# A mixture-of-experts loop that takes its token rows by transposing transfers instead of turning them on TensorE

## The reference

```python
x = x + tanh(g_xattn[0]) * _L0_xattn_ref(ctx_1024, _layernorm(x), ...)
x = x + tanh(g_ffn[0])   * _L0_ffn_ref(_layernorm(x), ...)      # experts
x = x + tanh(g_xattn[1]) * _L1_xattn_ref(_layernorm(x), ctx_1024, ...)
x = x + tanh(g_ffn[1])   * _L1_ffn_ref(_layernorm(x), w1, w2)

def _L0_ffn_ref(...):                       # 2048 tokens, 16 experts, 2 per token
    scores = sigmoid(x @ gate_w); _, selected = top_k(scores + expert_bias, 2)
    top_scores = scores of the two, divided by their sum
    shared = silu(x @ shared_gate_w) * (x @ shared_up_w) @ shared_down_w
    comb = zeros((T, E)).at[arange(T)[:, None], selected].add(top_scores)
    for e in range(16):
        g, u = split(x @ experts_gate_up[e], 2)        # 512 -> 2 x 256
        routed += comb[:, e:e + 1] * (silu(g) * u @ experts_down[e])   # 256 -> 512
    return shared + routed
```

## Time and profile before

| what | value |
|---|---|
| median of 3 runs | 1572.79 us (1571.97 to 1574.34) |
| profiled execution, its own time | 1561.98 us |
| its span | 1560.2 us |
| its mean granted TensorE clock | 0.972 |
| PE busy over the span | 1442.6 us, 92% |
| ACT, DVE, POOL busy | 967.2, 1111.0, 634.1 us |
| tile loads `e_xg` | 47 of 256 KB, median 2.7 us from issue to landing |

### The profile page before, as it was taken

One profiled execution on the slowest core, in us unless ns is written; L12 is line 12 of the kernel. 1 busy time (PEld: TensorE's weight loads), 2 busy tenths in 40 slices (PEclk: granted clock), 3 DMA queues, 4 the chain that ended last, 5 costly groups with the idle time before them and its releaser, 6 DMA issues. The chain is left out here.

```text
span 1560.2 us, 21493 instructions
## 1 busy us (share of the span) xinstructions
PE 1442.6 (92%) x6244; PEld 629.0 (40%) x6245; DVE 1111.0 (71%) x1628; ACT 967.2 (62%) x1544; POOL 634.1 (41%) x412
## 2 busy tenths in 40 slices
PE   5698988988988999999999999699999999999999
PEld 2344434434444444444444444123333333244444
DVE  7989999999996422222222488899999999647985
ACT  3999998999974001111111254478788788877764
POOL 0689799698981630064646565240000000000000
PEclk7799999999999999999999999699999999999999
DMA  5212314113205485357833566352322322220465
GB/s 188 72 48 84 94 55 119 44 56 109 75 15 197 155 203 187 128 182 238 288 128 100 187 211 163 108 175 74 96 75 73 94 77 73 60 108 14 88 141 122
DMA packets 137850, 183.45 MB, mean 118 GB/s; under 512 B 55491, under 2 KB 83523, under 8 KB 136755
## 3 DMA queue, kind: packets, MB, share of 16 engines
q1 hardware_dynamic: 113846, 123.83, 27.8%
q0 software_dynamic: 9024, 33.89, 7.0%
q10 hardware_dynamic: 14912, 24.89, 4.9%
HBM read 109.29 MB, written 54.92 MB: 105 GB/s over the span
## 5 line engine op out<-in xcount | busy, mean ns | idle before, releaser
L1916 DVE TENSOR_REDUCE a_mx<-a_s 128x2 f32<-128x1024 f32 x256 | 303.4, 1219 | 34.3 <-PE a_s L2033 31.4
L283 POOL TENSOR_TENSOR m_hs<-m_hs,m_C 128x1024 f32<-128x1024 f32 x128 | 301.5, 2377 | 53.9 <-DVE m_hs L508 53.2
L508 DVE TENSOR_TENSOR_SCAN m_hs<-m_dA,m_d 128x512 f32<-128x512 f32 x256 | 294.6, 1201 | 12.3 <-PE m_d L663 11.2
L663 PE MATMUL m_d<-ident_sb,m_dBuT 128*128 128x128 f32 x1024 | 160.2, 291 | 16.3 <-DVE m_hs L508 8.3
L389 ACT ACTIVATE m_dA<-m_dt,m_negA 128x512 f32<-128x512 f32 x256 | 167.8, 711 | 11.4 <-DMA m_dt<-m_dt 11.3
L663 PEld LDWEIGHTS m_d<-ident_sb,m_dBuT 128*128 128x128 f32 x1024 | 117.4, 146 | 141.5 <-DVE m_hs L508 69.7
L1357 PE MATMUL e_gu<-e_w,e_xgT 128*128 x376 | 169.1, 592 | 0.0
L367 ACT ACTIVATE m_dBuT<-m_dtuT,m_BT 128x512 f32<-128x512 f32 x241 | 157.8, 711 | 0.2
L2033 PE MATMUL a_s<-ring_sb 96*128 96x512 bf16 x512 | 152.3, 390 | 6.0 <-DVE a_mx L1916 4.3
L678 PE MATMUL m_y<-m_hs,m_fold 128*64 128x512 f32 x512 | 142.4, 637 | 3.6 <-POOL m_hs L283 3.6
L2307 POOL MEMSET f_ones<- 128x128 f32 x1 | 0.2, 204 | 343.7 <-POOLq L1500 343.7
(11 more groups left out here) (349 smaller groups left out, 2455.7 us busy)
## 6 DMA issues: line engine op xcount, KB each, us to landing
e_w<-in_ex_gu SPq DMA_DIRECT2D x16, 1024.0 KB, 6.3
ring_sb<-qk_dram SPq DMA_DIRECT2D x64, 192.0 KB, 3.1
xg_dram<-zeros_sb SPq DMA_DIRECT2D x47, 256.0 KB, 3.1
e_xg<-xg_dram ACTq DMA_DIRECT2D x47, 256.0 KB, 2.7
yg_dram<-attn_sb ACTq DMA_DIRECT2D x47, 256.0 KB, 2.1
m_C<-c_dram SPq DMA_DIRECT2D x64, 128.0 KB, 2.9
m_dt<-m_dt SPq DMA_DIRECT2D x64, 128.0 KB, 2.4
e_w<-in_ex_dn SPq DMA_DIRECT2D x16, 512.0 KB, 7.6
```

Source lines behind the costliest of these rows:

```text
L283: pool.tensor_tensor(hs[:, J % RH], hs[:, J % RH], C2[:, N % RC].unsqueeze(1).broadcast_to([P, 2, L]), ALU.mult).then_inc(s_hc, 1)
L508: dve.tensor_tensor_scan(hs[:, J % RH, h], dA[:, j % RA], pd[j % RD][:], 0.0, ALU.mult, ALU.add)\
L663: last = pe.transpose(pd[j % RD][:, t * P:(t + 1) * P], dBuT[:, N % 2, t, g], ident[:])
L1916: dve.tensor_reduce(mx[:, r % 2, h * TB + 2 * c:h * TB + 2 * c + 2], psc[c][:], AX.X, ALU.max)\
```

## The change

The rows reach `xgT` without PE. The scattered rows are stored as two planes of 16-bit numbers: POOL first copies every `xn` tile to a plane pair, the low halves of the 512 values and then the high halves (`planes`, 16 copies; tile 0 goes into `xgT`, tile t into the place of `xn` tile t - 1). `xg_dram` holds 1024 16-bit values in a row, the same 2 KB. ACT loads a tile by a transposing transfer, and its copy joins low and high halves into 512 float32 values. PE's `fetch` is gone; ACT copies tile j + 2 after the silu of tile j, where it had copied tile j + 1. ACT's loop is written out, PE's and DVE's stay loops. The four early loads become 16 pieces of 128 to 256 KB in another order (wk, context, wv, wq), each bound to a tile's end and to the landing of the piece before it.

```diff
+        xp = sb("xp", [P, 2, 2 * KD, P], U16)
-        xg = sb("xg", [P, 2, D])
+        planes = [xgT[:, 0].rearrange("p k t -> p (k t)")] + [xn[:, t] for t in range(NT - 1)]
@@ POOL, ahead of the scatter
+            for t in range(NT):
+                pool.wait_ge(s_xn, t + 1)
+                if t >= 1:
+                    pool.wait_ge(s_xt, t)
+                    pool.wait_ge(s_pl, t)
+                pool.tensor_copy(planes[t].bitcast(U16).rearrange("p (h d) -> p h d", h=2),
+                                 xn[:, t].bitcast(U16).rearrange("p (d h) -> p h d", h=2)).then_inc(s_pl, 1)
+            pool.wait_ge(s_pl, NT)
@@ POOL, loads of the projections' weights
-            for src, kn, width in ((a["ctxT"], KC, T), (a["wv"], KC, D), (a["wk"], KC, D), (a["wq"], KD, D)):
-                pool.dma_start(early[:, at:at + kn * width].rearrange("p (k e) -> p k e", k=kn),
-                               src.rearrange("(k p) e -> p k e", p=P)).then_inc(s_early, 16)
+            def load_early(n, name, k, width, col=0):
+                pool.wait_ge(s_y, NT + 1 + 2 * n)
+                if n >= 1:
+                    pool.wait_ge(s_early, 16 * n)
+                to = at[name] + k * (T if name == "ctxT" else D) + col
+                pool.dma_start(early[:, to:to + width], a[name][k * P:(k + 1) * P, col:col + width]).then_inc(s_early, 16)
+            EARLY = [("wk", k, D) for k in range(KC)] + [("ctxT", k, L, b * L) for b in range(B) for k in range(KC)] + \
+                [("wv", k, D) for k in range(KC)] + [("wq", k, D) for k in range(KD)]
             for m in range(2 * B):
+                first = 0 if m == 0 else KEYS_FROM + 2 * m
+                for n in range(first, min(KEYS_FROM + 2 * m + 2, len(EARLY))):
+                    load_early(n, *EARLY[n])
                 key_rows(m)
@@ ACT
             def load(j, par):
-                act.dma_start(xg[:, par], xg_dram[bass.ds(j, 1)].rearrange("o p d -> (o p) d"))\
-                    .then_inc(s_ld[par], 16)
+                act.dma_start_transpose(xp[:, par], xg_dram[j]).then_inc(s_ld[par], 16)
             def tile(j, par, more=True):
-                act.wait_ge(s_xt, NT + 1 + j)
+                act.wait_ge(s_ld[par], 16 * (j // 2 + 1))
                 act.wait_ge(s_gu, NB + j - 1)
-                act.activation(xgT[:, par], pxt[par][:], ACT.Copy).then_inc(s_xtc, 1)
+                act.activation(xgT[:, par].bitcast(U16).rearrange("p k (t h) -> p h k t", h=2),
+                               xp[:, par].rearrange("p (h k) t -> p h k t", h=2), ACT.Copy).then_inc(s_xtc, 1)
                 if more:
+                    act.wait_ge(s_xtc, NT + j + 1)
                     load(j + 2, par)
             tile(0, 0)
+            tile(1, 1)
             act.wait_ge(s_hm, NB)
             silu(0, 0)
-            tile(1, 1)
+            tile(2, 0)
             def pair(i):
                 for m in range(2):
                     silu(i * 2 + (m + 1), (m + 1) % 2)
-                    tile(i * 2 + (m + 2), m)
+                    tile(i * 2 + (m + 3), 1 - m)
                     store(i * 2 + m, m)
@@ PE
-            def fetch(j, par, nload):
...
             def step(i, m, before, e):
                 turn(i * 2 + (m - 1), (m - 1) % 2)
                 routed_up(i * 2 + m, m % 2, e)
-                if not last:
-                    fetch(i * 2 + (m + 1), (m + 1) % 2, (i + (m + 1) // 2) * 16 + 16)
                 routed_down(i * 2 + (m - 1), (m - 1) % 2, before)
             def key_block(b, f):
                 pe.wait_ge(s_kc, b * KD + (f + 1))
+                if f == 0:
+                    pe.wait_ge(s_early, b * 16 * KC + 16 * (KC + KC))
```

More of the change, by code:

```diff
@@ L14 @@
 U8 = mybir.dt.uint8
+U16 = mybir.dt.uint16
 ALU = mybir.AluOpType
@@ L199, in load_c @@
                     sp.dma_start(xg_dram[j].rearrange("p (c d) -> p c d", c=2),
-                                 zeros[:].unsqueeze(1).broadcast_to([P, 2, D // 2])).then_inc(s_zero, 16)
+                                 zeros[:].bitcast(U16).unsqueeze(1).broadcast_to([P, 2, D])).then_inc(s_zero, 16)
             def zeroed(N):
@@ L859, in moe @@
         s_slot = sem("slots_ready")
+        s_pl = sem("rows_in_halves")
         s_ej = sem("tile_experts")
@@ L959, in _ @@
                                             bass.IndirectOffsetOnAxis(ap=slot[:, k, t:t + 1], axis=0),
-                                            xn[:, t, :], None).then_inc(s_sct, 16)
+                                            planes[t].bitcast(U16), None).then_inc(s_sct, 16)
             pool.wait_ge(s_sct, 16 * 2 * NT)
@@ L967, in _ @@
             pool.wait_ge(s_y, NT)
[L968 to L972 removed]
+            at = {"ctxT": 0, "wv": KC * T, "wk": KC * T + KC * D, "wq": KC * T + 2 * KC * D}
+            def load_early(n, name, k, width, col=0):
[6 more added lines that the diff above has]
+                [("wv", k, D) for k in range(KC)] + [("wq", k, D) for k in range(KD)]
             def key_rows(m):
@@ L1087, in copy_key @@
                 act.activation(raw[:, f // 2, f % 2], pkm, ACT.Copy).then_inc(s_kc, 1)
-            with act.Fori(0, KEYS_FROM) as i:
+            for i in range((ST - 5) // 2):
                 pair(i)
[L1091 to L1094, removed]
-            for i in range(KEYS_FROM + KD * B, (ST - 5) // 2):
-                pair(i)
+                if 0 <= i - KEYS_FROM < KD * B:
+                    copy_key(*divmod(i - KEYS_FROM, KD))
             for j in range(ST - 3, ST):
                 silu(j - 1, (j - 1) % 2)
-                tile(j, j % 2, more=(j < ST - 2))
+                if j + 1 < ST:
+                    tile(j + 1, (j + 1) % 2, more=(j + 1 < ST - 2))
                 store(j - 2, j % 2)
@@ L1401, in _ @@
                 shared_down(t)
-            def fetch(j, par, nload):
-                pe.wait_ge(s_ld[par], nload)
-                if not (isinstance(j, int) and j < 2):
-                    pe.wait_ge(s_xtc, NT + j - 1)
-                for k in range(KD):
-                    last = pe.transpose(pxt[par][:, k], xg[:, par, k * P:(k + 1) * P], ident[:])
-                last.then_inc(s_xt, 1)
             def routed_up(j, par, e):
@@ L1423, in expert, with step, pair @@
                 return pe.value_load(ej[0:1, bass.ds(j, 1)], min_val=0, max_val=NE - 1)
-            def step(i, m, before, e, last=False):
+            def step(i, m, before, e):
                 turn(i * 2 + (m - 1), (m - 1) % 2)
                 routed_up(i * 2 + m, m % 2, e)
-                if not last:
-                    fetch(i * 2 + (m + 1), (m + 1) % 2, (i + (m + 1) // 2) * 16 + 16)
                 routed_down(i * 2 + (m - 1), (m - 1) % 2, before)
-            def pair(i, last=False):
+            def pair(i):
                 before, e1 = expert(i * 2), expert(i * 2 + 1)
@@ L1438, in pair @@
                 e2 = expert(i * 2 + 2)
-                step(i, 2, e1, e2, last)
-            fetch(0, 0, 16)
+                step(i, 2, e1, e2)
             shared_down(NT - 2)
@@ L1444, in _ @@
             routed_up(0, 0, expert(0))
-            fetch(1, 1, 16)
             shared_down(NT - 1)
@@ L1456, in _ @@
                 pair(i)
-            pe.wait_ge(s_early, 16 * 4)
             with pe.Fori(0, B) as b:
@@ L1463, in _ @@
                 pair(i)
-            pair((ST - 1) // 2 - 1, last=True)
+            pair((ST - 1) // 2 - 1)
             e = expert(ST - 1)
@@ L2107, in early_scores @@
                     scores(0, u // G4, u % G4, c)
-            pe.wait_ge(s_early, 16 * 4)
+            pe.wait_ge(s_early, 16 * 16)
             for t in range(12):
@@ L2607, in build @@
     c_dram = dram("c_dram", (B, NS, L))
-    xg_dram = dram("xg_dram", (ST, P, D))
+    xg_dram = dram("xg_dram", (ST, P, 2 * D), U16)
     yg_dram = dram("yg_dram", (ST, P, D))
```

2 lines of the change are left out of this document (1 added, 1 removed).

## The result

The changed kernel takes 1564.03 us in the median (1561.57 to 1567.92), the kernel before 1573.17 beside it: a ratio of 0.9942, interval 0.9929 to 0.9954. That is 9.1 us gained, where 22.1 were forecast, and 1564.03 lies just above the range.

A forecast was written before the change was run, and what follows sets the result against it. PE, busy 100 of 100 us in the loop, was taken as the bound. Turns saved 20.4 us and the stall 1.66, together 22.1, all other costs none: 1572.79 to 1550.7, called 1551; range 1547 to 1564.

The forecast's parts named there:

- The turns that go: PE's routed loop: 188 row turns vanish, each step falls from 5.81 to 5.37 us, saving 20.4 us.
- The stall that goes: PE's one wait in the loop, for a tile's rows at 579.43, goes with the 4 MB burst, saving 1.66 us.
- The product's chain: From up's end to the product's turn on PE, only the way down as cover: 0 to 5.9 us, taken as 0.
- ACT's duty: ACT's silu, copy, two issues and waits per loop step: 3.35 us of 5.37, so no cost.
- Landing: Transposing tile loads in the loop may take 8.9 us to land before it shows; expected cost none.
- The planes: POOL's 16 plane copies before the scatter take 18 us, done at about 503 in an idle gap; cost none.
- The start: First tile loads and first routed up, expected at 567.5; tables might stretch landing, loss 0 to 3.7 us, taken as 0.
- The end: POOL's last key work and stores before the next block: 27.7 us shrink to 26.0, still hidden; cost none.
- From the profile to the median: The 22.1 us saving on the profiled execution of 1561.98 was carried unchanged to the median, 10.81 us above it.
- Rival A: Part of the saving is eaten by product's chain, start and landings: gains 2 to 17 us, middle 1563; chance 0.18.
- B: Rival: ACT becomes the loop's bound through slow copy and issue, duty 6.43 us: +12.7 us, 1585; chance 0.08.
- C: Rival: the tile transfers become the loop's bound at 12.5 us landing: 1606; chance 0.06, together with a late scatter.

The follow-up runs named there:

- e16: The kernel before, unchanged, run again for a profile at the higher level: 1575.55 us, ratio 1.0014.
- e15: Changed kernel, sine table loads held until ACT copied the first two routed tiles, each table waiting for the one before: 1553.69 us, ratio 0.9860.
- e17: e15 run once more, unchanged: 1556.49 us, ratio 0.9894 to the kernel before.
- e3: The kernel before with only the early loads in 16 paced pieces: ratio 1.0003.
- e11: Changed kernel without the step of lead, ACT copying tile j + 1, not j + 2, behind silu j: 1572.91 us, ratio 0.9983.
- e2: The kernel before with only ACT's routed loop written out as straight code: ratio 0.9998.
- e12: The changed kernel, unchanged, as level for three kernels beside it on one chip: 1565.48 us, ratio 0.9937.
- e13: Changed kernel with the eight sine table loads held until ACT copied the first two routed tiles, on e12's chip: 1556.46 us, ratio 0.9880.
- e4: The changed kernel again, unchanged, for a second profile: 1560.34 us, ratio 0.9972.
- e6: Changed kernel with the early loads again as one burst of four transfers, 4 MB in all: 1562.67 us, ratio 0.9996.
- e1: Changed kernel with the eight sine table loads held until ACT copied the first two routed tiles: 1551.32 us, ratio 0.9911.
- e10: e1 run again: 1554.70 us, ratio 0.9847 to the kernel before.
- e8: Changed kernel, sine tables loaded one at a time at the ends of tiles 0 to 7, an early piece after every two: 1561.98 us, ratio 0.9909.

## Why the prediction was wrong, step by step

**The turns that go (20.4 us): right.** From the first to the last up e16 takes 294.7 us, e15 and e17 274.5: 20.2 less, which is 46 steps of 0.44.

**The stall that goes (1.66): small, not sure, and its cause misread.** It goes in the changed kernel, but e16 has none in its loop to lose, and e3 shows no gain. The prediction laid it, and the landing of 12.5 us, on the burst of early weights. That load was issued at 566.86, 8.8 us behind the first table and 7.6 ahead of the first early weight (574.42), and in e3, with no burst, the same load still takes 11.6. So 12.5 was mostly the mark of the tables, on a load that came 8.8 us behind them.

**The product's chain (0 of 0 to 5.9): right**, as the steps of 5.37 show; PE waits for it once in the loop of the changed kernel, 0.7 us, where ACT's silu was late behind the issue of 5.00 us.

**ACT's duty: right in the undisturbed step, low in its terms.** The copy is 1.35 us, not 1.06, the issue 1.25, not 0.95, a store's issue 0.59 in the median, not 0.36. That makes 0.38 + 1.35 + 1.25 + 0.59 + 0.6 = 4.2 us of 5.37, not 3.35; e11 shows that this fits only with the step of lead. On the issue, the Trainium skill's price by the tile ("DMA: Bandwidth & Descriptors", section "Why a DMA increments its semaphore by 16 and not by 1") was read as half of SP's 1.88; 1.25 is nearer to it than to a fixed price, and proves neither, since the engine differs and the page's figure is for a transpose within SBUF, where this one comes from DRAM.

**Landing: right in the loop's median, not at its ends.** 3.0 to 15.7 us with median 4.5, where the deadline was 8.9; the place at 717.87 us, with the longest of them, cost 1.7 us, which the prediction had at nothing. What the Trainium skill says of small pieces from HBM (same page, "Why small descriptors are slow (HBM only)") isn't tested by these rows: 3.0 us for a transfer from DRAM against 4.3 for one of twice the size within SBUF don't tell a fixed cost from a share.

**The planes: right.** 1.04 us each, done at 505.3, and the scatter starts at 517.79 because its slots came then. That is 2.5 us later than in the earlier trace rows, but e2, which has no planes, is later still (519.45). One small cost may hide in it: beside the plane copies some of DVE's short steps are longer, in e4 one of 1.30 us (line 1215) that takes 0.43 in the kernel before.

**The start (0 of 0 to 3.7): the step that failed.** The prediction saw the tables and bounded their effect by 12.5 us of landing. What the runs showed in its place is 18.5 to 22.4, with an issue that blocks ACT for up to 10.97 us, and behind the gap a stretch at a lower clock: 9.0 us in the medians (e12 less e13), 11.8 with e15. Three things were missed. The 12.5 was no bound: it belonged to a load 8.8 us behind the tables, and those issued 0.7 to 4 us behind them took 14.3 to 22.4. The loads were safe through 0.64 us of lead over the tables, and two transposing issues of 1.33 us each can't keep such a lead where plain ones of 0.4 can. And an issue isn't a fixed price on ACT: behind 2 MB just issued it took up to 10.97 us, and everything behind it on ACT waited with it.

**The end: 1.0 us short of right.** The next block starts 11.9 us behind the last up (862.01 to 873.95), and 11.0 before (864.97 to 875.93). This isn't scatter: e3, paced alone, has 12.0, e6, the changed kernel with the burst, 11.0. So the pacing of the early loads costs 1.0 us here, which the prediction had at nothing.

**From the profile to the median.** The prediction carried 22.1 us from an execution of 1561.98 to a median of 1572.79. That gap of 10.8 was a sign: e16 shows that such medians go with an ACT held through the scatter, which the profile of before didn't have. Term by term against e16 (own time 1571.59), the changed kernel's profile (1561.57) is: first up 584.21 against 578.54, +5.7; first to last up 277.8 against 294.7, -16.9 (20.2, less 1.6 for the slow up behind the gap and 1.7 for the place at 717.87); the rest of the span 697.7 against 696.5, +1.2, of which 1.0 is the end. Sum -10.0, as measured. At the lower level the change gives less, 5.0 us (e4), since there the plain loads of the kernel before are ahead of the tables; e1 gives 14.1.

Rival A named this outcome (part of the saving eaten, 1563 us), with the product's chain as its first cause; the chain cost nothing and the start nearly all of it. B and C didn't come about. Open are what holds ACT through the scatter, and why e17 gained 6.5 us less than e15 beside its own kernel before. The version with the most gain is e15, 1553.69 us: by the mean of e15 and e17 (23.4 and 16.9) 20 us under the kernel before, close to the 22.1 that was forecast for the change without this repair.

## What to carry to other kernels

When a load becomes one of another kind, list what else is issued within a few microseconds of it, in order, and ask who is ahead by how much: a lead of 0.64 us is no property of the kernel. Before a slow landing is laid on a burst, compare the times of issue: only what was issued before it landed can have slowed it. A big load that nobody needs yet belongs behind the small ones that somebody waits for, one piece in flight at a time, and not so late that it meets the loop in full step. If a profiled execution is 10 us off its median, the trace is of another case than the one to be predicted.

## What the hardware showed that was not expected

- The issue of a transposing transfer of 256 KB takes 1.25 us of ACT's queue with little under way, and 4.1 to 11.6 us in many cases within 21 us of the issue of 2 MB of tables or 4 MB of early loads (e10 4.11, e1 6.79, e12 10.71, e6 11.57). Beside experts' weights and early pieces it took 5.00 (changed kernel) and 5.89 us (e8).
- A 16-bit copy of 1024 elements in 4-byte steps takes 1.35 us on ACT, where the cast of the same count took 1.06.
- After a gap on PE of 5.9 to 12.6 us the next up takes 5.17 to 6.66 us instead of 3.60 (changed kernel, e12, e4); its stretch of 10 us has a granted clock of 0.66 in the changed kernel and 0.74 in e12, where the others have 1.00. In e16, with a gap of 2.0 us, it takes 3.60.
- ACT can stand idle through a scatter with its input ready; in e16, e12 and the changed kernel its silu then starts 45.2 to 45.7 us behind the first scatter, some 2.3 us after POOL has seen the scatter land, with no releaser that the profile names.
